# Mixing stage of an RWKV-like layer: gates made in step order inside the chunked scan, v copied through DRAM, states kept in PSUM

## The chip, the cores and the metric

One core of a Trainium2 chip runs the whole program. The metric is device time in microseconds (us) of one execution; the number for a kernel is the median of its runs. Engines: PE is TensorE (matmul), DVE is VectorE, ACT is ScalarE, POOL is GpSimd, SP is the engine that issues the transfers. SBUF is the working memory, PSUM the eight banks that matmuls write.

## The reference, cut to what matters

Inputs are 2 sequences of 1024 tokens with 128 channels, 16 heads of 8 channels. The first part ("mixing") computes, by token, projections of x mixed with the token before it, and from them gates; then a recurrence over the tokens of a sequence with one 8x8 state per head:

```
xx  = shift(x) - x ;  mix = x + xx*maa_x ;  lo = tanh(mix @ w1) @ w2 (4 parts)
xm  = x + xx*(lo + maa)                       # 4 versions: rg, wa, k, v
r, k, v, g ; w = -softplus(-(decay + w2)) - 0.5 ; a, ma, mk = sigmoid(...)
kk  = normalised(k + tanh(..)) by head ; b = -kk*a
k   = (k*ma + k*a*(1-ma)) * exp(w*mk)
step:  sa = s @ kk ;  s = s*exp(-exp(w)) + sa*b^T + v*k^T ;  y = s @ r
y   = groupnorm(y)*ln_w + ln_b + (sum r*k*faaaa)*v ;  out = (y*g) @ Wo
```

Then a layer norm, six layers of windowed attention and feed forward (the "stream"), and a last norm. Everything is float32.

## The kernel before, in words

The 2048 tokens are cut into 64 chunks (CHUNKS) of 32 steps (CHUNK). All chunks run side by side: a step of the scan works on a tile of 128 partitions (head and column) by 512 elements (8 state rows by 64 chunks). Each chunk starts from a zero state and carries two states: p=0, the state that this chunk adds, and p=1, the propagator that says what the chunk does to any start. The starts are chained afterwards. The program is a row of phases; each is a block in which every engine has its own hand-written order, with semaphores between them, and a barrier and a clearing of all the phase's semaphores (line 83) between two phases.

- **Projections** (`build_projections`). SP loads the constants; DVE, PE and ACT wait for all of them (`loaded`). Data lies by token. The matmuls follow one list `order`, in four groups of 512 tokens, over 8 PSUM banks in turn; ACT and DVE empty the banks.
- **Gates** (`build_gates`). On whole 128x2048 tiles: squares and norms of kk (line 289, 311, 331), softplus (290 to 294), a running sum of the decay by `tensor_tensor_scan` (328), decay and growth (300, 301), the gain of k (326, 341, 343, 345, 348), and the four operands of a step, `a_step`, `b_step`, `r_step`, `k_step`, rearranged from token order to step order (351 to 386). Last, 32 matmuls with `spread` (321) copy each row of v over its head's partitions, and 32 DVE products (372) make `vk`, 128 partitions by 16384 elements, the v k^T of every step.
- **Scan** (`build_scan`). 32 steps. Per step, DVE has eight instructions: `times_a` for p=0 and p=1 (line 435), `times_r` for p=1 (460), `add_vk` (441), `times_b` for both (445) and `renew` for both (454). POOL makes `times_r` for p=0 (497). PE multiplies by `headones` (`product_u`, 506) and collects y with 8 matmuls (`products_y`, 514); ACT copies y out (533). The states alternate between two SBUF tiles. A float32 matmul is two passes in the trace.
- **Mix output** (`build_mix_output`). The starts are chained, y is completed, normalised, gated and projected.
- **Stream** and **final**. Not touched by the change.

Of the kernel before, what the change touches and what calls it, by code (L numbers as in the profile page):

```python
# [21 lines left out]
F32 = mybir.dt.float32  # L22
# [68 lines left out]
def mix_inputs(sb):  # L91

    t = {}
    for name, shape in (("xT", (P, N)), ("vecs", (P, 16)), ("ident", (P, P)), ("w_lo", (P, P)), ("w_maa", (P, P)),
                        ("w_r", (P, P)), ("w_g1", (P, P)), ("w_g2", (P, P)), ("w_xwa", (P, P)), ("w_k", (P, P)),
                        ("w_xk", (P, 64)), ("w_v", (P, P)), ("w_second", (P, P)), ("w_xk2", (64, P)),
                        ("w_o", (P, P)), ("headones", (P, P)), ("spread", (P, HS * P)), ("collect", (P, HS * P)),
                        ("headmask", (P, HEADS)), ("rowmask", (P, HS))):
        t[name] = sb(name, shape)
    return t  # L100
# [3 lines left out]
V_MAAX, V_MAA, V_DECAY, V_AAAAA, V_MISCA, V_MISCK, V_FAAAA, V_LNW, V_LNB, V_ONE, V_YEPS, V_LNEPS = \  # L104
    0, 1, 5, 6, 7, 8, 9, 10, 11, 12, 13, 14

AAA_AT, MA_AT = 64, 96
MK_AT = 32


def build_projections(nc, a, t, loads, banks):

    with PhaseSignals(nc) as sems, ExitStack() as ctx:
        def sig(name, **kw):
            return Signal(sems, name, **kw)

        xx, mix, lo, gt, h1, h2 = (ctx.enter_context(nc.sbuf_tensor(n, [P, N], F32))
                                   for n in ("xx", "mix", "lo", "gt", "h1", "h2"))
        xm = [ctx.enter_context(nc.sbuf_tensor(f"xm{g}", [P, N], F32)) for g in range(4)]
        xT, vecs = t["xT"], t["vecs"]  # L120
        loaded = sig("p_loaded")
        loaded_x = sig("p_loaded_x")
        xx_made, mix_made, lo_made, gt_made = sig("xx_made"), sig("mix_made"), sig("lo_made"), sig("gt_made")
# [4 lines left out]
        a_made, ma_made, mk_made, kk_made = sig("a_made"), sig("ma_made"), sig("mk_made"), sig("kk_made")  # L128
# [18 lines left out]
        MAA, FIRST = ("maa0", "maa1", "maa2", "maa3"), ("r", "g1", "xwa", "k", "xk", "v")  # L147
        SECOND = ("g2", "z", "a", "ma", "kk", "mk")
# [12 lines left out]
        small = [n for n in loads if n != "xT"]  # L161

        @block.sync
        def _(sp):
            sp.dma_start(t["vecs"][:, :], a["vecs"]).then_inc(loaded.sem, 16)
            sp.dma_start(xT[:, :], a["xT"]).then_inc(loaded_x.sem, 16)
            for name in small:
                if name != "vecs":
                    sp.dma_start(t[name][:, :], a[name]).then_inc(loaded.sem, 16)

        @block.tensor
        def _(pe):
            pe.wait_ge(loaded.sem, 16 * len(small))
            for i, (name, j) in enumerate(order):
                w, moving, (r0, r1), ready, _ = products[name]
                pe.wait_ge(ready.sem, ready.after(j))
                if i >= 8:
                    before, at = order[i - 8]
                    freed = products[before][4]
                    pe.wait_ge(freed.sem, freed.after(at))  # L180
# [4 lines left out]
        def _(dve):  # L185
            dve.wait_ge(loaded_x.sem, 16)
            dve.wait_ge(loaded.sem, 16 * len(small))

            for s in range(B):
                lo_, hi = s * T, (s + 1) * T  # L190
                nc.vector.tensor_scalar(xx[:, lo_:lo_ + 1], xT[:, lo_:lo_ + 1], -1.0, None, ALU.mult).then_inc(xx_made.sem, 1)
                nc.vector.tensor_tensor(xx[:, lo_ + 1:hi], xT[:, lo_:hi - 1], xT[:, lo_ + 1:hi],
                                        ALU.subtract).then_inc(xx_made.sem, 1)
            dve.wait_ge(xx_made.sem, 2 * B)
            for j in range(GROUPS):
                nc.vector.scalar_tensor_tensor(out=mix[:, g_of[j]], in0=xx[:, g_of[j]], scalar=vecs[:, V_MAAX:V_MAAX + 1],
                                               in1=xT[:, g_of[j]], op0=ALU.mult, op1=ALU.add).then_inc(mix_made.sem, 1)

            def mix_in(j):

                for g in range(4):
# [4 lines left out]
                for g in (2, 3):  # L206
                    dve.wait_ge(xm_scaled[g].sem, j + 1)
                    nc.vector.tensor_tensor(xm[g][:, g_of[j]], xm[g][:, g_of[j]], xT[:, g_of[j]], ALU.add).then_inc(xm_made[g].sem, 1)
# [6 lines left out]

            for j in range(3):
                mix_in(j)
            raw_kk(0)
            mix_in(3)
            for j in range(1, GROUPS):  # L220
                raw_kk(j)

        @block.gpsimd
        def _(pool):
            for j in range(GROUPS):
# [4 lines left out]

        @block.scalar
        def _(act):
            nc.scalar.preload_act_table_set("sigmoid_and_others")
            act.wait_ge(loaded.sem, 16 * len(small))
# [8 lines left out]
                     "v": ([(t["v"], whole, ACT.Copy, None)], v_made), "g2": ([(t["g"], whole, ACT.Copy, None)], g_made),  # L243
                     "z": ([(t["z"], whole, ACT.Identity, V_DECAY), (t["w"], whole, ACT.Sigmoid, V_DECAY)], z_made),
                     "a": ([(t["a"], whole, ACT.Sigmoid, V_AAAAA)], a_made),
                     "ma": ([(t["ma"], whole, ACT.Sigmoid, V_MISCA)], ma_made),
                     "mk": ([(t["mk"], whole, ACT.Sigmoid, V_MISCK)], mk_made)}
            for name, j in order:
                if name not in reads:
                    continue  # L250
# [7 lines left out]
def build_gates(nc, t, banks, vk, last_decay):  # L258

    with PhaseSignals(nc) as sems, ExitStack() as ctx:  # L260
        def sig(name, **kw):
            return Signal(sems, name, **kw)

        vecs = t["vecs"]
        e, norm = (ctx.enter_context(nc.sbuf_tensor(n, [P, N], F32)) for n in ("gate_e", "kk_inverse"))
        gain, summed, segment, decay, growth = (vk[:, N * i:N * (i + 1)] for i in range(5))
        sq, k_step = t["xT"], t["xT"]
        squared, floored, ss_product, log_made = sig("kk_squared"), sig("floored"), sig("ss_product"), sig("log_made")
        kk_norm, kk_unit, kk_gated, soft, act_step = sig("kk_norm"), sig("kk_unit"), sig("kk_gated"), sig("soft"), sig("act_step")
        gain_made, k_scaled, key_gain, k_stepped = sig("gain_made"), sig("k_scaled"), sig("key_gain"), sig("k_stepped")  # L270
        segmented, decay_summed, decay_made, growth_made = sig("segmented"), sig("decay_summed"), sig("decay_made"), sig("growth_made")
        steps_made, v_spread, vk_made = sig("steps_made"), sig("v_spread"), sig("vk_made")
        block = ctx.enter_context(nc.Block())
        g_of = [slice(GROUP * j, GROUP * (j + 1)) for j in range(GROUPS)]
        RATE = float(np.exp(-0.5))
        PER = GROUP // CHUNKS

        def by_token(ap):

            return ap.rearrange("p (c l) -> p l c", l=CHUNK)  # L280

        def by_step(ap):

            return ap.rearrange("p (l c) -> p l c", c=CHUNKS)

        @block.scalar
        def _(act):
            nc.scalar.preload_act_table_set("natural_log_exp_and_others")
            nc.scalar.activation(sq[:, :], t["kkraw"][:, :], ACT.Square).then_inc(squared.sem, 1)
            nc.scalar.activation(e[:, :], t["z"][:, :], ACT.Abs).then_inc(act_step.sem, 1)  # L290
            act.wait_ge(act_step.sem, 1)
            nc.scalar.activation(e[:, :], e[:, :], ACT.Exp, scale=-1.0).then_inc(act_step.sem, 1)
            act.wait_ge(act_step.sem, 2)
# [1284 lines left out]
```

## Time and profile before

| | us |
|---|---|
| median of 3 runs | 2137.53 (2132.94 to 2140.84) |
| profiled execution, its own time | 2134.84 |
| span of the profiled execution | 2132.8 |
| projections, from the start to the first instruction of the gates | 69.12 |
| gates | 97.67 |
| scan | 169.66 |
| mix output | 116.64 |
| stream and final | 1679.71 |

The span is the time from the first to the last instruction; the rest of the execution's time, 2.0 us, lies around it. Phases follow each other with a barrier, so a phase that gets shorter by some time moves all that follows it by the same time.

### The profile page before, as it was taken

What the parts mean: (1) busy time and instruction counts of PE and PEld (TensorE: products, weight loads), DVE (VectorE), ACT (ScalarE), POOL (GpSimd) and SP (SyncE); (2) the same over time, 40 slices, a digit from 0 to 9 for tenths busy, and PEclk for the clock granted to TensorE, in tenths of its full rate; (3) what the DMA queues carried; (4) which work ended last, traced back from release to release, by engine and by line L of the source; (5) the groups of instructions that cost most, each with busy time, mean ns of one, the idle gap of its engine ahead of it and who ended that gap; (6) DMA issues with size and microseconds to landing.
All of it is one profiled execution on the core that took longest, in us unless ns stands there. A gap on an engine that the chain in (4) does not pass through costs nothing. (4 is left out here: it accounts for less than half of the span.)

```text
span 2132.8 us, 74062 instructions
## 1 busy us (share of the span) xinstructions
PE 1907.6 (89%) x31300; PEld 1318.9 (62%) x31300; DVE 1569.4 (74%) x2888; ACT 1221.0 (57%) x2361; POOL 1161.1 (54%) x682
## 2 busy tenths in 40 slices
PE   6576777948999999999999999999999999999984
PEld 2113556825677766667776776766777677776662
DVE  4768997347787787777877778777787777877743
ACT  4500001126677676776766767667677676776751
POOL 1401221018667666666666767666676666766630
PEclk9788998559999999999999999999999999999996
DMA  1000000033222222322223222232222322322220
GB/s 56 0 0 1 1 0 20 1 128 72 66 67 68 65 72 65 111 66 64 72 69 110 69 64 72 71 105 67 67 72 74 102 68 64 73 63 62 69 53 20
DMA packets 84859, 128.49 MB, mean 60 GB/s; under 512 B 26736, under 2 KB 32304, under 8 KB 83504
## 3 DMA queue, kind: packets, MB, share of 16 engines
q1 hardware_dynamic: 84528, 123.75, 22.8%
q8 instruction: 247, 4.05, 0.8%
q14 instruction: 84, 0.69, 0.1%
HBM read 21.94 MB, written 1.05 MB: 11 GB/s over the span
## 5 line engine op out<-in xcount | busy, mean ns | idle before, releaser
L961 POOL TENSOR_TENSOR qk<-qk,rnorm 128x1024 f32<-128x1024 f32 x192 | 361.4, 1904 | 368.9 <-ACT rnorm L1186 292.6
L955 POOL TENSOR_TENSOR qk<-qk,turnedhalf 128x1024 f32<-128x1024 f32 x192 | 454.8, 2369 | 142.8 <-DVE turnedhalf L1312 142.8
L1308 DVE TENSOR_TENSOR qk<-bank,gains 128x512 f32<-128x512 f32 x384 | 262.2, 683 | 235.1 <-ACT squares L1176 220.6
L1012 PE MATMUL bank<-wqkv,x 128*128 128x512 f32 x768 | 377.8, 595 | 22.0 <-DMA qk_gain<-in_qk_gain 20.1
L1176 ACT ACTIVATE squares<-bank 128x512 f32<-128x512 f32 x384 | 232.6, 606 | 166.0 <-PE bank L1012 163.2
L1312 DVE TENSOR_TENSOR turnedhalf<-bank,gains 128x256 f32<-128x256 f32 x768 | 285.3, 412 | 0.0
L1223 ACT ACTIVATE o_T<-bank 128x512 f32<-128x512 f32 x192 | 104.3, 599 | 229.7 <-PE bank L1076 229.6
L1318 DVE TENSOR_REDUCE rnorm<-squares 128x16 f32<-128x1024 f32 x192 | 230.6, 1201 | 2.8
L1076 PEld LDWEIGHTS bank<-p_T,v_win 64*64 64x64 f32 x12288 | 189.8, 135 | 58.0 <-issue 57.7
L1025 PEld LDWEIGHTS bank<-st_ident,qk 128*128 128x128 f32 x1536 | 179.0, 142 | 58.3 <-issue 52.2
L1017 PE MATMUL bank<-wqkv,x 128*128 128x512 f32 x384 | 202.0, 607 | 7.2 <-DVE turnedhalf L1312 6.7
L1076 PE MATMUL bank<-p_T,v_win 64*64 64x32 f32 x12288 | 201.2, 220 | 5.2 <-issue 5.1
L1025 PE MATMUL bank<-st_ident,qk 128*128 128x128 f32 x1536 | 193.6, 275 | 1.5 <-issue 1.5
L979 POOL TENSOR_TENSOR probs<-probs,total 128x1024 f32<-128x1024 f32 x96 | 183.0, 1906 | 16.2 <-DVE total L1340 16.2
L1012 PEld LDWEIGHTS bank<-wqkv,x 128*128 128x128 f32 x768 | 138.3, 191 | 84.1 <-issue 70.6
L1089 PE MATMUL bank<-o_T,wo 128*128 128x256 f32 x768 | 175.4, 382 | 2.5 <-DVE xf L1379 2.5
L1106 PE MATMUL bank<-xn_T,w 128*128 128x256 f32 (+1 forms) x576 | 163.1, 393 | 13.7 <-ACT xn_T L1242 3.3
L1089 PEld LDWEIGHTS bank<-o_T,wo 128*128 128x128 f32 x768 | 146.9, 192 | 43.1 <-issue 25.2
L1056 PE MATMUL bank<-k_T,q_T 64*32 64x64 f32 x12288 | 159.1, 225 | 15.7 <-issue 14.4
L1056 PEld LDWEIGHTS bank<-k_T,q_T 64*32 64x32 f32 x12288 | 138.9, 105 | 42.2 <-issue 39.4
L1358 DVE SCALAR_TENSOR_TENSOR ff_T<-bank,b,gate_T 128x256 f32<-128x256 f32 x144 | 64.7, 477 | 134.9 <-PE bank L1106 134.9
L1216 ACT ACTIVATE p_T<-bank 128x512 f32<-128x512 f32 x192 | 104.7, 594 | 84.8 <-PE bank L1025 84.3
(200 smaller groups left out, 3080.9 us busy)
## 6 DMA issues: line engine op xcount, KB each, us to landing
v_win<-v_tok SPq DMA_DIRECT2D x1536, 64.0 KB
wqkv<-in_wqkv SPq DMA_DIRECT2D x6, 1536.0 KB
wo<-in_wo SPq DMA_DIRECT2D x6, 512.0 KB
w<-in_w SPq DMA_DIRECT2D x6, 341.0 KB
w<-in_w SPq DMA_DIRECT2D x6, 192.0 KB
xT_sb<-in_xT SPq DMA_DIRECT2D x1, 1024.0 KB, 5.7
x_tok_sb<-in_x_tok SPq DMA_DIRECT2D x1, 1024.0 KB, 4.8
tables<-in_tables SPq DMA_DIRECT2D x2, 512.0 KB, 4.5
```

The lines of the kernel that those rows point to most:

```text
L955: nc.gpsimd.tensor_tensor(out=qk[n % 2][:, half], in0=qk[n % 2][:, half], in1=turnedhalf[:, half], op=ALU.add).then_inc(rot_added.sem, 1)
L961: nc.gpsimd.tensor_tensor(out=by_head(qk[u][:, half]), in0=by_head(qk[u][:, half]), in1=rnorm[u][:, AH * i:AH * (i + 1)].unsqueeze(2).to_b ...
L1012: nc.tensor.matmul(QK_BANKS[i][:, :], shifted_tokens(x, n, P), layer_cols(wqkv, n, 3 * INNER, 512 * i, 512), start=True, stop=True).then_i ...
L1017: nc.tensor.matmul(V_BANKS[i][:, :], shifted_tokens(x, n, P), layer_cols(wqkv, n, 3 * INNER, 2 * INNER + 512 * i, 512), start=True, stop=T ...
L1025: mm = nc.tensor.transpose(outs[i // 4][:, P * (i % 4):P * (i % 4 + 1)], source[:, P * i:P * (i + 1)], ident[:, :])
L1056: mm = nc.tensor.matmul(S_BANKS[p][at:at + WINDOW, 2 * WINDOW * a_:2 * WINDOW * (a_ + 1)], q_T[rows, a_, at:at + WINDOW], k_T[rows, a_, ke ...
L1076: mm = nc.tensor.matmul(S_BANKS[p][DH * side:DH * (side + 1), P * q + at:P * q + at + WINDOW], v_win[n % 2][rows, w, DH * a_:DH * (a_ + 1) ...
L1089: mm = nc.tensor.matmul(FF_BANK[:, 0:PT], layer_cols(wo, n, INNER, C * i, C), o_T[:, i, :], start=(i == 0), stop=(i == PAIRS - 1))
L1176: nc.scalar.activation(squares[:, 512 * i:512 * (i + 1)], QK_BANKS[i][:, :], ACT.Square).then_inc(squared.sem, 1)
L1308: nc.vector.tensor_tensor(by_head(qk[u][:, cols]), src, cos.to_broadcast([P, 8, DH]), ALU.mult).then_inc(rotated.sem, 1)
L1312: nc.vector.tensor_tensor(by_head(turnedhalf[:, cols])[:, :, to], src[:, :, frm], sin[:, :, to].to_broadcast([P, 8, half]), ALU.mult).then ...
L1318: nc.vector.reduce_sum(rnorm[n % 2][:, AH * h:AH * (h + 1)], by_head(squares[:, INNER * h:INNER * (h + 1)]), AX).then_inc(ss_made.sem, 1)
```

## The change

Everything of the mixing before the output is put in step order (chunk fastest, then step), by laying x out so on the host. Then a group of 512 columns is eight steps of all chunks (STEPS = 8), and the operands of the first eight steps can be made without the rest.

- `build_gates` goes. Its work is done by group inside `build_scan`: for group 0 ahead of the scan, and for groups 1 to 3 in between the steps of the group before (`in_step`, with a list `stages` for ACT, DVE and PE). In place of the scan over the decay (328), POOL adds the columns of one step to the next, 31 small additions of 128x64 in the projections (`sums`). The gain of k is made in the projections (`gain`), with an additional sigmoid of the negated input (`unheld`) on ACT.
- The 32 `spread` matmuls and the 32 DVE products go. v is stored to a DRAM tensor `v_dram` and read back with each row repeated over the 8 partitions of its head, 16 transfers of 128 KB per group, into `v_rep0` or `v_rep1`; POOL multiplies by k step by step (`times_k`), two steps ahead.
- In the scan the two states stay in two PSUM banks and are renewed in place. DVE loses `add_vk`; POOL adds v k to the product of b (`add_vk`), between `times_b` and `renew0`. ACT copies state 0 to SBUF for POOL's `times_r`.
- In the projections DVE, PE and ACT wait only for three loads (`FIRST_LOADS`); PE waits for the others ahead of its fifth matmul. The order of the products is changed (v first, `SECOND` = kk, a, mk, ma, z, g2). `spread`, 512 KB, is not loaded.
- In the mix output `bonus` is written by token with a stride, and two tiles take space of `v_rep0`.

```
-        small = [n for n in loads if n != "xT"]
+        rest = [n for n in loads if n not in FIRST_LOADS]
...
+            for j in range(GROUPS):
+                sp.wait_ge(v_made.sem, j + 1)
+                sp.dma_start(v_dram[:, g_of[j]], t["v"][:, g_of[j]]).then_inc(v_stored.sem, 16)
...
+                    for h in range(HEADS):
+                        rows = slice(HS * h, HS * (h + 1))
+                        sp.dma_start(v_rep[rows, :, :, :].rearrange("p i l c -> p i (l c)"),
+                                     v_dram[rows, g_of[0]].unsqueeze(0).to_broadcast([HS, HS, GROUP])).then_inc(v_copied.sem, 16)
...
+            def sums(j):
+                pool.wait_ge(z_made.sem, z_made.after(j))
+                for l in range(max(STEPS * j, 1), STEPS * (j + 1)):
+                    if l > 1:
+                        pool.wait_ge(summed.sem, l - 1)
+                    w = [t["w"][:, CHUNKS * m:CHUNKS * (m + 1)] for m in (l - 1, l)]
+                    nc.gpsimd.tensor_tensor(out=w[1], in0=w[0], in1=w[1], op=ALU.add).then_inc(summed.sem, 1)
...
 # scan, ACT
+            squares(0); absolutes(0); log_z(0); inverse_norm(0); decays(0); key_gain(0); growths(0); decays_again(0)
+            stages = ((squares, absolutes), (log_z, inverse_norm), (decays,), (), (), (key_gain,), (growths,), (decays_again,))
+            for l in range(CHUNK):
+                in_step(l, stages)
+                copy_state(l)
+                if l >= 2:
+                    read_y(l - 2)
 # scan, DVE
+            stages = ((), (), (soft_sum, unit_kk), (soft_gate, gated_kk), (soft_growth, steps_a), (steps_k,), (steps_b,), (steps_r,))
+            for l in range(CHUNK):
+                if l:
+                    times_b(0, l)
+                times_b(1, l)
+                renew1(l)
+                if l + 1 < CHUNK:
+                    times_a(1, l + 1)
+                renew0(l)
+                if l + 1 < CHUNK:
+                    times_a(0, l + 1)
+                times_r(l)
+                in_step(l, stages)
...
+            def renew0(l):
+                if l:
+                    dve.wait_ge(vk_added.sem, l + 1)
+                    dve.wait_ge(s_copied.sem, l)
+                    nc.vector.tensor_tensor(S_BANKS[0][:, :], S_BANKS[0][:, :], ubvk[:, :], ALU.add).then_inc(s_new[0].sem, 1)
 # scan, POOL
+            def add_vk(l):
+                pool.wait_ge(ub_made[0].sem, l)
+                pool.wait_ge(vk_made.sem, l + 1)
+                if l >= 2:
+                    pool.wait_ge(s_new[0].sem, l)
+                nc.gpsimd.tensor_tensor(out=rows(ubvk[:, :]), in0=rows(ub[:, 0, :]), in1=vk_of(l), op=ALU.add).then_inc(vk_added.sem, 1)
+            for l in range(CHUNK):
+                if l:
+                    add_vk(l)
+                    times_r(l - 1)
+                if l + AHEAD < CHUNK:
+                    times_k(l + AHEAD)
 # scan, PE
+            stages = ((sums_of_squares,), (), (), (), (), (), (), ())
             for l in range(CHUNK):
                 if l + 1 < CHUNK:
+                    product_u(1, l + 1)
                     product_u(0, l + 1)
                 if l:
                     products_y(l - 1)
+                in_step(l, stages)
 # mix output
-                nc.vector.tensor_tensor(bonus[:, g_of[j]], banks[4 + j % 2][:, :], t["v"][:, g_of[j]],
+                out = bonus_by_token[:, :].rearrange("p (c l) -> p l c", l=CHUNK)[:, STEPS * j:STEPS * (j + 1), :]
+                nc.vector.tensor_tensor(out, by_step(banks[4 + j % 2][:, :]), by_step(t["v"][:, g_of[j]]),
```

## Rows read from the trace of the kernel before

**Rows 1.** Busy time by phase: stretch, length, each engine's busy us (instructions), granted clock, DMA.
```profile
0.00:69.12 69.12, 44.79 (x136) 15.53 (x136) 25.83 (x36) 36.48 (x62) 10.23 (x13) 0.98 0.14 43
69.12:166.79 97.67, 60.81 (x72) 15.86 (x72) 72.82 (x49) 18.33 (x11) 24.75 (x5) 0.78 0.00 0
166.79:336.45 169.66, 125.49 (x640) 84.79 (x640) 162.38 (x260) 12.73 (x64) 41.19 (x32) 0.96 0.00 1
336.45:453.09 116.64, 89.83 (x388) 75.20 (x388) 59.81 (x169) 26.35 (x62) 11.58 (x6) 0.63 0.03 10
```

**Rows 2.** Timeline of the projections: start us, us, engine, line, what.
```profile
10.47 0.43 SPq L169 DMA_DIRECT2D rowmask_sb<-in_rowmask  x1
...
14.50 0.15 DVE L191 TENSOR_SCALAR xx<-xT_sb 128x1 f32<-128x1 f32 x1 [14.50 <-DMA rowmask_sb<-in_rowmask]
...
17.91 5.37 PE L181 MATMUL bank<-mix,w_lo_sb 128*128 128x512 f32 x8 [17.91 <-DVE mix L196]
...
64.86 0.75 ACT L255 ACTIVATE ma_sb<-bank,vecs_sb 128x512 f32<-128x512 f32 x1
65.43 0.76 ACT L255 ACTIVATE mk_sb<-bank,vecs_sb 128x512 f32<-128x512 f32 x1
69.16 2.84 DVE L326 TENSOR_SCALAR vk_sb<-a_sb 128x2048 f32<-128x2048 f32 x1 [4.34 <-PEq L83]
```

**Rows 3.** Transfers of the first 60 us: count, size, median us to landing.
```profile
xT_sb<-in_xT SPq DMA_DIRECT2D x1, 1024.0 KB, 5.7
...
w_lo_sb<-in_w_lo SPq DMA_DIRECT2D x1, 64.0 KB, 4.8
```

**Rows 4.** Groups of DVE instructions in the gates: busy us, mean ns, idle before.
```profile
L341 DVE TENSOR_TENSOR vk_sb<-vk_sb,ma_sb 128x2048 f32<-128x2048 f32 x1 | 6.7, 6652 | 0.0
...
L351 DVE TENSOR_TENSOR xT_sb<-k_sb,vk_sb 128x2048 f32<-128x2048 f32 x1 | 4.0, 4045 | 0.0
...
L336 DVE TENSOR_TENSOR gate_e<-gate_e,z_sb 128x2048 f32<-128x2048 f32 x1 | 2.3, 2293 | 0.1
```

**Rows 5.** Timeline of one steady step of the scan, DVE and POOL.
```profile
189.09 0.68 DVE L435 TENSOR_TENSOR sc_m<-sc_ahead,z_sb 128x512 f32<-128x512 f32 x1
...
191.50 1.28 DVE L445 TENSOR_TENSOR sc_ub<-bank,ma_sb 128x512 f32<-128x512 f32 x2
...
191.71 1.27 POOL L497 TENSOR_TENSOR xT_sb<-state_sb,w_sb 128x512 f32<-128x512 f32 x1 [3.69 <-DVE sc_sw L441]
192.70 0.83 DVE L454 TENSOR_TENSOR state_sb<-sc_ahead,sc_ub 128x512 f32<-128x512 f32 x1
...
194.06 0.68 DVE L435 TENSOR_TENSOR sc_m<-state_sb,z_sb 128x512 f32<-128x512 f32 x1
```

**Rows 6.** Timeline of the last step of the scan, POOL and DVE.
```profile
328.30 1.65 POOL L497 TENSOR_TENSOR xT_sb<-state_sb,w_sb 128x512 f32<-128x512 f32 x1 [1.23 <-DVE state_sb L454]
328.74 1.75 DVE L460 TENSOR_TENSOR xT_sb<-sc_ahead,w_sb 128x512 f32<-128x512 f32 x1
```

**Rows 7.** Timeline of the mix output: a matmul and its reader, two dependent DVE instructions.
```profile
354.71 3.79 PE L676 MATMUL bank<-kkraw_sb,headones_sb 128*128 128x512 f32 x8
355.77 0.69 DVE L599 TENSOR_TENSOR kkraw_sb<-bank,v_sb 128x512 f32<-128x512 f32 x1 [2.02 <-PE bank L676]
...
422.58 0.69 DVE L636 TENSOR_TENSOR z_sb<-z_sb,kkraw_sb 128x512 f32<-128x512 f32 x1
...
423.30 0.69 DVE L638 TENSOR_TENSOR z_sb<-z_sb,g_sb 128x512 f32<-128x512 f32 x1
```

**Rows 8.** Busy time at the start of the scan, columns as in the first group.
```profile
172.00:182.00 10.00, 6.90 (x8) 2.62 (x9) 7.35 (x12) 0.00 (x0) 2.48 (x2) 0.51 0.00 0
182.00:189.00 7.00, 5.83 (x37) 4.37 (x35) 6.68 (x11) 0.72 (x4) 1.33 (x2) 1.00 0.00 0
```

**Rows 9.** Groups of POOL instructions, shapes kept apart.
```profile
L379 POOL MEMSET vk_sb<- 128x64 f32 x1 | 1.2, 1170 | 0.1
L943 POOL TENSOR_TENSOR centring<-st_ident,mean_ones 128x128 f32<-128x128 f32 x1 | 0.5, 456 | 0.0
```

More of the change, by code:

```diff
@@ L199, in mix_in @@
             def mix_in(j):
-                for g in range(4):
+                for g in (3, 0, 1, 2):
                     dve.wait_ge(done[f"maa{g}"].sem, j + 1)
@@ L288, in _ @@
             nc.scalar.preload_act_table_set("natural_log_exp_and_others")
[L289 to L293, printed above, removed]
-            nc.scalar.activation(e[:, :], e[:, :], ACT.Ln, bias=vecs[:, V_ONE:V_ONE + 1]).then_inc(act_step.sem, 1)
@@ new lines, in absolutes, with log_z @@
+            def absolutes(j):
+                z = t["z"][:, g_of[j]]
+                if j:
+                    act.wait_ge(soft.sem, soft.after(j - 1, 1))
+                nc.scalar.activation(relu_z[:, :], z, ACT.Relu, scale=-1.0).then_inc(z_relu.sem, 1)
+                nc.scalar.activation(z, z, ACT.Abs).then_inc(z_abs.sem, 1)
+                act.wait_ge(z_abs.sem, j + 1)
+                nc.scalar.activation(z, z, ACT.Exp, scale=-1.0).then_inc(z_exp.sem, 1)
+            def log_z(j):
+                act.wait_ge(z_exp.sem, j + 1)
+                if j:
+                    act.wait_ge(r_made.sem, j)
+                nc.scalar.activation(Z_BANK[:, :], t["z"][:, g_of[j]], ACT.Ln, bias=vecs[:, V_ONE:V_ONE + 1]).then_inc(z_log.sem, 1)
@@ new lines, in decays, with key_gain, growths @@
+            def decays(j):
+                nc.scalar.activation(decay[:, CHUNKS + GROUP * j:CHUNKS + GROUP * (j + 1)], t["w"][:, g_of[j]], ACT.Exp,
+                                     scale=-RATE).then_inc(decay_made.sem, 1)
+            def key_gain(j):
+                act.wait_ge(soft.sem, soft.after(j))
+                nc.scalar.activation(Z_BANK[:, :], Z_BANK[:, :], ACT.Exp).then_inc(gain_made.sem, 1)
+            def growths(j):
+                act.wait_ge(k_made.sem, j + 1)
+                nc.scalar.activation(Z_BANK[:, :], t["w"][:, g_of[j]], ACT.Exp, scale=RATE).then_inc(growth_made.sem, 1)
@@ new lines, in decays_again, with copy_state @@
+            def decays_again(j):
+                act.wait_ge(b_made.sem, j + 1)
+                nc.scalar.activation(Z_BANK[:, :], t["w"][:, g_of[j]], ACT.Exp, scale=-RATE).then_inc(decay_again.sem, 1)
+            def copy_state(l):
+                if l + 1 < CHUNK:
+                    act.wait_ge(s_a[0].sem, s_a[0].after(l))
+                else:
+                    act.wait_ge(s_new[0].sem, s_new[0].after(l))
+                if l >= 2:
+                    act.wait_ge(s_r[0].sem, s_r[0].after(l - 2))
+                nc.scalar.activation(s_copy[:, l % 2, :], S_BANKS[0][:, :], ACT.Copy).then_inc(s_copied.sem, 1)
@@ new lines, in read_y @@
+            def read_y(l):
+                act.wait_ge(y_product.sem, y_product.after(l))
+                for p, y in enumerate((t["y"], t["zy"])):
+                    out = y[:, :].rearrange("p (c l) -> p l c", l=CHUNK)[:, l:l + 1, :]
+                    nc.scalar.activation(out, Y_BANKS[l % 2][:, CHUNKS * p:CHUNKS * (p + 1)].unsqueeze(1), ACT.Copy).then_inc(y_read.sem, 1)
+            squares(0)
+            absolutes(0)
+            log_z(0)
+            inverse_norm(0)
+            decays(0)
@@ L1509, in layouts @@
     out["headones"] = same.astype(f)
-    out["spread"] = np.concatenate([(same & (row == i)[:, None]).astype(f) for i in range(HS)], 1)
     out["collect"] = np.concatenate([(same & (row == i)[None, :]).astype(f) for i in range(HS)], 1)
```

535 lines of the change are left out of this document (276 added, 259 removed).

## Prediction, made before the changed kernel was run

> **What bounds the kernel now.** I read the busy time by phase first, then the timeline of each phase that the change touches. Phases are separated by barriers, so the question is what each phase costs. Gates and scan together take 267.3 of the 2132.8 us [rows 1]; 1796.4 us after them are untouched but for four instructions. No engine fills the gates: DVE is busy 72.8 of 97.7 us, PE 60.8, and they take turns. The first half is DVE beside POOL (below), the second a chain of matmul and product for vk. The reader is to see there that a DVE instruction with both inputs in SBUF, 2293 ns long by itself, took 6652 ns while POOL worked [rows 4]. In the scan, DVE is busy 162.4 of 169.7 us [rows 1]: eight instructions a step, 4.97 us from step to step [rows 5]. So DVE bounds the scan, and PE, ACT and POOL have room. The projections start late: DVE's first instruction at 14.50 us was released by the last of all loads [rows 2], and ACT is the last engine to end, at 66.19, 2.9 us before the gates.
>
> **Projections.** Three loads are needed instead of all. xT lands 5.7 us and w_lo 4.8 us after its issue [rows 3]; issued first and third (about 0.74 and 1.7), both are there by about 6.9. From DVE's start to PE's first matmul were 3.4 us [rows 2]; with xx made by group these are an edge, 448 columns (0.6) and one mix (0.75), about 2.1. PE starts at 9.0 instead of 17.91: -8.9. The other loads had landed by 14.5 [rows 2] and the first four matmuls take 5.4 us, so PE's new wait ahead of its fifth costs nothing. ACT has one sigmoid more per group; two starts are 0.57 apart [rows 2], and only in the last two groups does ACT run without a gap: +1.0, less 0.4 since v no longer waits in the line. POOL's sums are new: 128x128 took 456 ns [rows 9] and 128x512 1.27 us [rows 5], so 0.0021 us an element and about 0.32 for 64, with the handoff to itself 0.4. The first three groups lie beside other work; the last eight, 3.2 us, start after w's last sigmoid, 0.6 before ACT ends: +2.6. Bounds: 0.3 each gives +1.8; the one POOL instruction on 64 columns took 1170 ns [rows 9], beside a DVE instruction, and at that price groups 2 and 3 both run late, +13. I take 0.4, since nearer shapes say so. Six more semaphores to clear: gaps of 1.3 us after the scan (14 semaphores) and 2.9 after the projections (42, [rows 2]) say 0.06 each, +0.4. Together -5.3; the scan's phase begins at 63.8 instead of the gates' at 69.12.
>
> The stores and copies of v are out of the way, I think. SP has nothing else to issue in either phase; a load of 1 MB landed in 5.7 us [rows 3]. Group 0's 2 MB have over 40 us, group 1's are needed six steps into the scan (some 43 us), those of groups 2 and 3 are released when the steps that read the buffer are done and have seven steps (36 us) each. If the 16 transfers of a group came one after another at 5.7 us each, they would need 91 us: rival 4.
>
> **Gates in front of the scan.** Only 512 columns are made ahead: ACT table load 1.3; square, Relu, Abs, Exp, Ln at 0.57 to 0.6 (3.1); the floor, Ln and Exp of the norm (1.9, dependent) and the decay (0.6); then DVE's steps_a, times_a, gated_kk, steps_k (2.6), growth on ACT and steps_b (1.3), decay again and steps_r (1.4), with 1.5 us of handoffs between them and for the cold square-sum matmul: 12.7 us to the first `times_b`. The price of the small DVE instructions is that of 128x512 with a PSUM input, 0.69 [rows 7]. This replaces 97.67 us and some 3 us of setting up the scan.
>
> **The steady step.** Let T be the end of `times_b` for p=0. On DVE independent instructions start 0.60 apart, dependent ones 0.72 [rows 5, 7]. `times_b` p=1 starts at T-0.09, renew1 at T+0.64, `times_a` p=1 at 1.37 to 2.06, renew0 at 1.97 to 2.66, `times_a` p=0 at 2.70 to 3.39. PE takes it 0.06 later, and its reader starts 1.06 after the matmul [rows 7]: the next `times_b` starts at 4.51 and ends at 5.20. `times_r` fits before it (3.30 to 3.99). So the period is 5.20, set by the loop through PE, and DVE idles 0.5 us, against 4.97 before. The wait that the change adds, renew0 on POOL's `add_vk`: POOL starts 0.13 after its input and takes 1.27 [rows 5], done at T+1.40, while renew0 can't start before 1.97 in DVE's order: nothing, by 0.57 us. Behind renew0 are queued `times_a` p=0 and with it everything; each us beyond that cover costs a us per step. POOL's three instructions take 4.0 of 5.2 us. PE's y matmuls (2 us) wait for POOL's `times_r`, end at T+6.3 and are not needed by the `product_u` of the next step before T+7.3. ACT's copy of the state has 3 us of slack.
>
> The gates of the next group are nine DVE instructions: none in two steps of eight, one in three (0.60, it fills the idle 0.5), two in three (+0.6 each). Three groups: 9 x 0.6 = +5.4. At the start PE's granted clock is 0.5: before, it was so for some 15 us of thinly used PE, and 1.00 from 182 on [rows 8]; the first three steps cost 5.5, 6.6 and 7.1 instead of 5.2, +3.6. So 31 x 5.20 + 5.4 + 3.6 = 170.2 us from the first step to the last, 7.4 to the last read of y, and 2.8 for the barrier (39 semaphores). The phase takes 12.7 + 170.2 + 7.4 + 2.8 = 193.1 instead of 267.3: -74.2. Bounds of the period: 4.8 if the loop through PE is 0.4 shorter (the second pass overlaps more), -12; the upper is the writing of PSUM by DVE, which no row shows. Reading PSUM costs nothing that the rows show (`times_b` from a bank starts its twin 0.60 later, like the others). The nearest row of a slowed instruction is a renewal of 0.83 against 0.68 [rows 5]; 0.15 on the six instructions of the loop is 0.9 a step, +28. I take no surcharge, since `times_b` is nearest.
>
> The page "VectorE: DVE Perf Modes" of the Trainium skill (section "The TRN2 errata — SBUF-src ops pay a fixed extra latency per instruction") speaks against states in PSUM: it gives a DVE instruction that reads PSUM 120 cycles of fixed cost against 58 from SBUF. At its 0.96 GHz that is 0.065 us, on six instructions 0.39 a step, an estimate of +12 for the scan. The trace doesn't agree: two `times_b`, which read a bank, take 1.28 together [rows 5].
>
> **Mix output.** The four bonus products are written with a stride. A fully strided instruction took 4045 against 2293 ns [rows 4], so 0.3 more per 512 columns: +1.2.
>
> **Sum.** -5.3 - 74.2 + 1.2 = -78.3, from the profiled execution's own 2134.84: 2056.5. The median of the runs is 2.7 above that execution; I put half of it on top: **2058**.
>
> **The rivals.**
> 1. Forecast, 2058, own range 2045 to 2072. Chance 0.68.
> 2. DVE pays for PSUM operands, or the loop is longer by as much: from 2058 + 12 (0.4 a step) to 2058 + 28. For it: nobody wrote PSUM from DVE in this scan; against: `times_b`. 2070 to 2086, chance 0.14.
> 3. POOL's sums cost 1.2 us each, +10: 2068. For: the 1170 ns row; against: DVE held POOL there. Or the v copies are some us late in each group. Chance 0.10.
> 4. The other side: POOL and DVE exclude each other. POOL now works 4 of 5.2 us in the scan, and in the last step before, both slowed each other, 1.65 against 1.27 and 1.75 against 0.68 [rows 6]. If they took strict turns, a step would be 4.6 us of DVE plus 3.8 of POOL, 8.4: +99 on 31 steps, 2157. It decides from 7.7 us a step (78.3/31 more than 5.2). Against it: two `times_b`, one input in a bank, ran under POOL's 1.27 without getting longer [rows 5], and now each DVE instruction of a step has an input in a bank. The same sign comes from v copied one transfer at a time, 91 us a group against some 40, three times 50. Together 0.05.
> 5. Faster than my range: the period is 4.6 (DVE's own sum) and the projections save more, 2036. Chance 0.03.
>
> Beyond the ends of the range lies about 0.1 on each side: 2044 to 2086. What a measurement here can tell from no change is 0.5%, 11 us: faster 0.93, within it 0.02, slower 0.05.
>
> **What would show it.** First PE matmul at 9 us; the scan's phase from 64 to 257; first `times_b` 13 us into it; 5.2 us steady steps in the last eight, with DVE waiting for PE ahead of `times_b` p=0 and not for POOL ahead of renew0; renew0 and renew1 at 0.69; POOL at 1.27; the stream as long as before. A wait for POOL at renew0, renewals over 0.75, or a DMA releasing `times_k` would make it wrong.

## The result, and the profile after

| | before | after |
|---|---|---|
| median of the runs, us | 2135.24 (2125.82 to 2140.84, 4 runs) | 2053.78 (2050.26 to 2054.72, 4 runs) |
| profiled execution, its own time | 2134.84 | 2050.26 |
| projections | 69.12 | 66.86 |
| gates and scan | 267.33 | 193.95 |
| mix output | 116.64 | 118.43 |
| stream and final | 1679.71 | 1669.26 |

The ratio is 0.962, 95% interval 0.9582 to 0.9658: faster, and 2053.78 lies 4.2 below the forecast of 2058. The busy time by phase of the kernel after answers to [rows 1]; the four rows are projections, scan with its gates, mix output, and stream with final.

```profile
0.00:66.86 66.86, 45.11 (x136) 15.38 (x136) 37.46 (x53) 39.66 (x65) 23.30 (x43) 0.95 0.42 84
66.86:260.81 193.95, 141.41 (x646) 86.90 (x646) 168.62 (x262) 57.31 (x145) 118.06 (x95) 0.92 0.25 33
260.81:379.24 118.43, 90.20 (x388) 75.41 (x388) 60.78 (x169) 26.32 (x62) 11.57 (x6) 0.62 0.03 10
379.24:2048.50 1669.26, 1582.03 (x30064) 1122.41 (x30064) 1248.83 (x2374) 1126.06 (x2163) 1073.01 (x627) 0.98 0.29 74
```

DVE's 168.6 busy us of 193.95 say that it is nearly full and yet not the only bound. The mixing ends at 379.24 instead of 453.09, which is -73.85 where the forecast's sum had -78.3. The other -10.4 of this pair of profiles lie in the stream, whose code is the same; what they are, the first experiment tells.

The timeline of the projections of the kernel after, the same places as [rows 2]:

```profile
6.07 0.15 DVE L202 TENSOR_SCALAR vecs_sb<-vecs_sb 128x1 f32<-128x1 f32 x1 [6.07 <-DMA w_lo_sb<-in_w_lo]
...
8.01 2.90 PE L196 MATMUL bank<-x,w_lo_sb 128*128 128x512 f32 x3 [8.01 <-DVE x L213]
...
58.73 1.15 ACT L306 ACTIVATE g_sb<-bank 128x512 f32<-128x512 f32 x1
59.02 3.97 POOL L271 TENSOR_TENSOR w_sb<-w_sb 128x64 f32<-128x64 f32 x8 [0.72 <-ACT w_sb L313]
66.94 0.11 DVE L468 MEMSET decay<- 128x64 f32 x1 [6.50 <-PEq L83]
```

DVE starts when w_lo is there, and PE 9.9 us earlier than before. But ACT ends at 59.88, only 6.3 earlier: it needs 49.7 us from its first `lo` (10.16) to its end, against 46.1 before. POOL's last sums end later still, at 62.99, and the barrier takes the rest. Two groups of ACT instructions say why ACT needs longer, the copy of g that is now written with a stride and the additional sigmoid (`unheld`, which lies in the tile `x`); the third line is the copy of g in the kernel before:

```profile
L306 ACT ACTIVATE g_sb<-bank 128x512 f32<-128x512 f32 x4 | 4.5, 1118 | 0.0
L302 ACT ACTIVATE x<-bank,vecs_sb 128x512 f32<-128x512 f32 x4 | 2.8, 696 | 0.0
```

```profile
L255 ACT ACTIVATE g_sb<-bank 128x512 f32<-128x512 f32 x4 | 2.4, 603 | 0.3
```

One steady step of the scan, timeline of the kernel after (it answers to [rows 5]). L531 is `times_b`, L526 `times_a`, L537 `renew0`, L544 `renew1`, L551 `times_r`; L597 is POOL's `add_vk`, L633 PE's `product_u`:

```profile
218.68 1.29 DVE L531 TENSOR_TENSOR sc_ub<-bank,mk_sb 128x512 f32<-128x512 f32 x2 [0.62 <-PE bank L633]
219.45 1.27 POOL L597 TENSOR_TENSOR sc_ubvk<-sc_ub,v_rep 128x512 f32<-128x512 f32 x1 [1.57 <-DVE sc_ub L531]
220.01 0.70 DVE L544 TENSOR_TENSOR bank<-bank,sc_ub 128x512 f32<-128x512 f32 x1
220.68 1.27 POOL L604 TENSOR_TENSOR sc_m<-sc_copy,r_sb 128x512 f32<-128x512 f32 x1
220.74 0.69 DVE L526 TENSOR_TENSOR sc_m<-bank,z_sb 128x512 f32<-128x512 f32 x1
221.35 0.69 DVE L537 TENSOR_TENSOR bank<-bank,sc_ubvk 128x512 f32<-128x512 f32 x1
...
222.07 0.69 DVE L526 TENSOR_TENSOR sc_m<-bank,z_sb 128x512 f32<-128x512 f32 x1
222.68 0.68 DVE L551 TENSOR_TENSOR sc_m<-bank,r_sb 128x512 f32<-128x512 f32 x1
...
222.82 1.12 PE L633 MATMUL bank<-sc_m,headones_sb 128*128 128x512 f32 x2 [0.21 <-DVE sc_m L526]
...
223.98 0.69 DVE L531 TENSOR_TENSOR sc_ub<-bank,mk_sb 128x512 f32<-128x512 f32 x1 [0.62 <-PE bank L633]
```

Read it as a loop: `times_b` p=0 (218.68), its `renew0` (221.35), `times_a` p=0 (222.07), the matmul (222.82), the next `times_b` (223.98). The period is 5.30. The only wait of DVE is for PE, 0.62. POOL's sum `add_vk` is ready at 220.72, 0.63 before `renew0` starts. Groups of DVE instructions in the scan's phase, mean ns of one:

```profile
L531 DVE TENSOR_TENSOR sc_ub<-bank,mk_sb 128x512 f32<-128x512 f32 x63 | 40.6, 684 | 11.2 <-PE bank L633 10.9
L544 DVE TENSOR_TENSOR bank<-bank,sc_ub 128x512 f32<-128x512 f32 x32 | 22.4, 700 | 1.1
...
L537 DVE TENSOR_TENSOR bank<-bank,sc_ubvk 128x512 f32<-128x512 f32 x31 | 21.4, 690 | 0.1
```

A renewal, which reads a bank and writes one, takes 690 to 700 ns; `times_b`, which only reads one, takes 684.

A step did not get shorter: 5.30 us against 4.97 in the kernel before. The phase without its front takes 181.5 us, the scan before took 169.66. So all of the 73.4 us that gates and scan became shorter come from the gates, 97.67 us before and now 12.5 in front of the first `times_b` and some 5 inside the steps (gates_ahead below). No run gave DVE its `add_vk` back or kept the `spread` matmuls and their products; how the gain divides among these edits is not shown.

### The profile page after: what moved, and what is told of

Its sections match the earlier page's. It is cut to its first block and busy times, and to the rows that moved or that the text cites. A ratio compares the mean times of both kernels' runs of the same rounds, so it can differ in the third digit from the quotient of the medians.

```text
span 2048.5 us, 74276 instructions
## 1 busy us (share of the span) xinstructions
PE 1858.8 (91%) x31234; PEld 1300.1 (63%) x31234; DVE 1515.7 (74%) x2858; ACT 1249.4 (61%) x2435; POOL 1225.9 (60%) x771
```

## The experiments

Each is the kernel after with one edit, but for the first (none) and for v_16_twice, best and best2 (several). The scan's phase is from its first instruction to the first of the mix output.

**before_again and after_again: both kernels once more, in rounds.** No edit.

> The kernel before once more. The stretch from the start of the stream to the end was 1679.7 us in the first trace of before and 1669.3 in that of after, with the same instructions. If this is a spread between executions, this trace shows another length of that stretch, somewhere from 1665 to 1690, with the mixing as before (453.1 to 1 us). If instead the change made the stream shorter, this trace shows 1679.7 within 2 us again.

> The changed kernel once more. The mixing ends again at 379.2 within 1 us. Spread theory: the stretch after it differs from 1669.3 by some us either way. Rival (the change shortens the stream): 1669.3 within 2 us.

Measured: the kernel before 2137.61 us (ratio to itself 0.9994, 0.9974 to 1.0014), the kernel after 2060.31 us, ratio 0.9623 (0.9578 to 0.9667). In the profiled executions the stream took 1678.3 and 1679.0 us; the scan's phase of the kernel after took 192.72, from 66.47 on. Windows of the second profile of the kernel after:

```profile
66.47:259.19 192.72, 141.12 (x646) 86.64 (x646) 168.47 (x262) 57.31 (x145) 118.01 (x95) 0.92 0.26 33
377.49:2056.50 1679.01, 1588.84 (x30064) 1127.53 (x30064) 1248.38 (x2374) 1125.97 (x2163) 1072.79 (x627) 0.98 0.29 74
```

What follows: before_again alone came out as its rival had it (1678.3 is within 2 us of 1679.7); after_again decides, since the same kernel's stream now took 9.8 us more than in its first profile. The mixing repeats within 1.8 us, not within the 1 us expected. The stream's 1669.26 was the shortest of fourteen profiles (the thirteen others: 1672.8 to 1682.6), and in the second pair the stream was no shorter with the change. So the 10.4 us are spread between executions; that a part of a few us is not, these profiles can't exclude. In the second pair the mixing is 76.0 us shorter (it ends at 453.5 and 377.5).

**all_loads: DVE waits for every load again.**

```
             dve.wait_ge(loaded_first.sem, 16 * len(FIRST_LOADS))
+            dve.wait_ge(loaded.sem, 16 * len(rest))
```

> Undoes the early start alone: DVE's first instruction waits for all loads again. My theory: the last load lands at about 12.9 us (issue at 9.6, 2.8 to landing), DVE starts there and not at 6.1, and all of the 6.8 us reach the start of the scan's phase, 73.7 instead of 66.9. Rival (PE or ACT bound the projections, the early start is absorbed): 67 to 70.

Measured: 2062.73 us, ratio 0.9651 (0.962 to 0.9683). DVE's first instruction, timeline:

```profile
13.03 0.15 DVE L203 TENSOR_SCALAR vecs_sb<-vecs_sb 128x1 f32<-128x1 f32 x1 [13.03 <-DMA rowmask_sb<-in_rowmask]
```

PE starts at 14.97 instead of 8.01, and the scan's phase begins at 72.65 instead of 66.86: of 7.0 us at the start 5.8 reach the end of the projections, nearer to the theory's 73.7 than to the rival's 67 to 70. So in the traces the short list of loads is worth some 6 us, more than all that the projections won (2.26). The totals can't tell it (2060.31 for the kernel after in the same round, and the intervals overlap).

**pool_twice: POOL makes v k plus the product twice.**

```
+                nc.gpsimd.tensor_tensor(out=rows(ubvk[:, :]), in0=rows(ub[:, 0, :]), in1=vk_of(l), op=ALU.add).then_inc(once.sem, 1)
+                pool.wait_ge(once.sem, l)
                 nc.gpsimd.tensor_tensor(out=rows(ubvk[:, :]), in0=rows(ub[:, 0, :]), in1=vk_of(l), op=ALU.add).then_inc(vk_added.sem, 1)
```

> POOL makes the sum of v k and the product of b twice in each of 31 steps, one after the other, so vk_added comes 1.26 us later. My theory, the addition is hidden behind DVE's order with 0.6 us to spare: the period goes from 5.30 to 5.96, the scan's phase gets 20 us longer (31 x 0.66). Rival (the addition is already what renew0 waits for): +1.26 a step, +39. Rival (the loop is not through POOL at all): below +3.

Measured: 2089.15 us, ratio 0.9768 (0.9729 to 0.9806), 28.8 more than the kernel after in the same round; scan's phase 221.2, +27.2. The timelines of DVE and of POOL in one step:

```profile
214.72 1.27 POOL L598 TENSOR_TENSOR sc_ubvk<-sc_ub,v_rep_sb 128x512 f32<-128x512 f32 x1 [1.47 <-DVE sc_ub L532]
216.06 1.26 POOL L600 TENSOR_TENSOR sc_ubvk<-sc_ub,v_rep_sb 128x512 f32<-128x512 f32 x1
...
217.36 0.70 DVE L538 TENSOR_TENSOR bank<-bank,sc_ubvk 128x512 f32<-128x512 f32 x1 [0.67 <-POOL sc_ubvk L600]
...
227.01 1.29 DVE L532 TENSOR_TENSOR sc_ub<-bank,mk_sb 128x512 f32<-128x512 f32 x2 [0.97 <-PE bank L636]
```

POOL's second sum adds 1.34, of which the cover of 0.63 hides a part and `renew0` waits 0.67. The undisturbed step is 6.06, +0.76, where the theory had +0.66; 31 steps make 23.6, where it had 20. So the theory is nearer than its rivals, +39 and below +3. Of the other 3.6 us, 1.4 lie in the last step, where DVE has no `times_a` ahead of `renew0`, which waits 1.39 for POOL. The other 2.2 lie in the steps, and go with PE's granted clock: it was 0.89 from 216 to 232 and 0.91 from 232 to 250, where the kernel after had 1.00, and the step that ends at 227.01, with 0.97 of waiting for PE, took 7.01. That the clock made these steps long is read from the trace, no run held it. POOL's own instructions stay at 1.27 with DVE at work all along, so the two don't take turns (the prediction's fourth rival).

**gates_ahead: all four groups of gates before the first step,** on ACT, DVE and PE (the same for DVE's and PE's lists):

```
-            squares(0)
...
-            decays_again(0)
-            stages = ((squares, absolutes), (log_z, inverse_norm), (decays,), (), (), (key_gain,), (growths,), (decays_again,))
+            for j in range(GROUPS):
+                for stage in (squares, absolutes, log_z, inverse_norm, decays, key_gain, growths, decays_again):
+                    stage(j)
+            stages = ((),) * STEPS
```

> The gates of all four groups are made ahead of the first step, with the same instructions, none in the scan. My theory, each group is a chain of 9.0 us between ACT and DVE (from its Ln to steps_r, as group 0 shows), and in the scan it costs only 3 x 3 x 0.6 us of DVE: +27 ahead, -5.4 in the steps, the scan's phase +22. Rival (the gates in the steps cost DVE their full 27 x 0.6 = 16 us, or delay the loop): +27 - 16 = +11 or less.

Measured: 2080.07 us, ratio 0.9739 (0.9721 to 0.9756); scan's phase 218.18, +24.2. The first `times_b` comes 41.6 us into the phase instead of 12.5; the rest takes 176.6 instead of 181.5. Hence three groups of gates cost 29 us in front of the scan (theory 27) and 5 inside it. They fit there because DVE has 0.62 idle in a step: a step with one of their DVE instructions still takes 5.30, one with two takes 5.78 at full clock. A third of the gain on gates and scan (24.2 of 73.4) would be lost without this overlap.

**v_twice: every copy of v a second time, into a tile that nobody reads.**

```
...
+                    sp.dma_start(dump[part, :, :, :].rearrange("p i l c -> p i (l c)"),
+                                 v_dram[part, g_of[j]].unsqueeze(0).to_broadcast([HS, HS, GROUP])).then_inc(v_again.sem, 16)
```

> Each copy of v for groups 1 to 3 is made twice, the second time into a tile that nobody reads, so the transfers' traffic in the scan doubles. My theory, the copies have over 10 us of slack in every group: the same steps, scan's phase within 1 us. Rival (the copies are just in time, or slow other things down in SBUF): times_k waits for a DMA at steps 6, 14 or 22, over 3 us each.

Measured: 2130.01 us in one execution, some 75 more; scan's phase 270.6, +76.6. The theory (within 1 us) failed, and its rival came true: three waits of over 20 us each. What POOL waited for, in total, times, longest:

```profile
POOL v_rep L596 <- DMA v_rep<-v_by_step: 49.3, 2, 28.2
POOL v_rep_sb L596 <- DMA v_rep_sb<-v_by_step: 30.6, 1, 30.6
```

Windows of the kernel after, while the copies of group 1 run and behind them (the last two columns are DMA share and GB/s):

```profile
66.86:99.90 33.04, 17.88 (x50) 8.31 (x50) 24.05 (x38) 15.62 (x27) 13.07 (x11) 0.68 0.51 64
99.90:121.94 22.04, 17.81 (x80) 11.26 (x80) 21.23 (x35) 5.33 (x15) 14.32 (x13) 0.92 0.00 1
```

A group's 2 MB take 31 to 33 us, at 64 GB/s and with half of the DMA engines' time. Group 3 was issued at 166.13, had landed at 197.1 and was first read at 206.01: 9 us of slack. Group 2 had less: the last of its bytes moved at 155.2 and it was first read at 161.98, some 6 us. Group 1 had 18 (99.9 and 117.79). Doubling the copies uses all of it up. The prediction had put this cost among the hidden ones by the rate of another transfer; it was hidden, but just.

**v_16 and v_16_twice: 8 copies of 256 KB over all partitions in place of 16 over 8,** and the same doubled as above (into the unread tile).

```
-                for h in range(HEADS):
-                    part = slice(HS * h, HS * (h + 1))
-                    sp.dma_start(vk[j % 2][part, :, :, :].rearrange("p i l c -> p i (l c)"),
-                                 v_dram[part, g_of[j]].unsqueeze(0).to_broadcast([HS, HS, GROUP])).then_inc(v_copied.sem, 16)
+                for i in range(HS):
+                    sp.dma_start(vk[j % 2][:, i, :, :].rearrange("p l c -> p (l c)"), spread_row(v_dram, i, j)).then_inc(v_copied.sem, 16)
```

where `spread_row` takes row i of each of the 16 heads and repeats it over the head's 8 partitions; the copies of group 0 in the projections likewise.

> The kernel after, with each group's 2 MB of v copied by 8 transfers of 256 KB, each over all 128 partitions (outermost dimension 16 heads), instead of 16 transfers of 128 KB, each over 8 partitions. Theory (the copies after run on half of the DMA engines, share 0.53, 31 us a group, because the outermost dimension is 8): the share while they run is near 1.0 and a group lands 15 to 18 us after its first issue; SP's wait for group 3 falls from 23 us to 8 to 10. The step doesn't depend on it: the scan's phase stays at 193 to 195 us and the whole within 0.5% of after. Rival (the DRAM side or the small rows set the rate): 28 to 33 us a group and a share that rises without the rate rising.

> The same as v_16, and every copy of groups 1 to 3 issued a second time into a tile that nobody reads. The doubled copies at half the engines cost +75 us in the scan's phase, by POOL's wait at times_k. Theory (the missing engines were the reason, and there is now twice the slack): a doubled group lands in 30 to 36 us, as a single one did after, and the scan's phase stays within 3 us of 194. Rival (the rate is set by something else than the number of engines): again +50 to +75 us, POOL's times_k released by DMA.

Measured: 2062.29 and 2055.73 us, one execution each; scan's phase 193.10 and 193.59. Windows of v_16 during the copies of group 3, and one of v_16_twice at the same place:

```profile
168.00:172.00 4.00, 2.79 (x17) 1.77 (x16) 3.90 (x7) 1.75 (x4) 3.31 (x3) 1.00 0.91 191
172.00:176.00 4.00, 3.77 (x20) 2.46 (x20) 3.31 (x7) 1.54 (x5) 2.43 (x3) 1.00 0.85 165
```

```profile
178.00:182.00 4.00, 3.46 (x20) 2.24 (x18) 3.30 (x6) 2.46 (x6) 2.43 (x3) 1.00 0.86 193
```

The rate goes from 64 GB/s to between 165 and 193 and the share from 0.53 to some 0.9; group 3 lands 14.3 us after its issue instead of 31. Doubled copies now cost nothing (76.6 us of the scan's phase before): POOL waits for no DMA, and a doubled group 3 lands 24.1 us after its issue, where 30 to 36 were expected. The time doesn't fall by it, since the copies were hidden; the slack grows. That the old copies left half of the DMA engines idle agrees with a rule of the Trainium skill ("DMA: Bandwidth & Descriptors", section "Rules for kernel authors"): an outermost dimension of c below 16, a broadcast of c copies for instance, confines a transfer to at most c engines. Here c was 8. The rate rose by almost three and not by two, which the rule doesn't explain; the transfers were also half as many and twice as long, and no run parts the two.

**p0_first: p=0 is served first,** since the loop goes through it (PE's two `product_u` likewise).

```
                 renew1(l)
-                if l + 1 < CHUNK:
-                    times_a(1, l + 1)
                 renew0(l)
                 if l + 1 < CHUNK:
                     times_a(0, l + 1)
+                    times_a(1, l + 1)
```

> DVE renews state 0 and multiplies it by a before it does so for state 1, and PE takes the product of p=0 first; no instruction more or less. My theory, the period of 5.30 is the loop b, renew1, a1, renew0, a0, PE: with a1 out of the loop it ends 0.5 earlier, 4.8 in steps without gates, 5.25 and 5.85 in those with one or two of their instructions: the scan's phase -7.6 us. Now renew0 starts when POOL's sum arrives, with no cover left. Rival (POOL's sum, or PE's second product, is then as late as what it replaces): -1 to +3.

Measured: 2051.62 us, ratio 0.9609 (0.9586 to 0.9631); scan's phase 185.77, -8.2. Timeline of one step of DVE and POOL:

```profile
213.39 0.69 DVE L531 TENSOR_TENSOR sc_ub<-bank,mk_sb 128x512 f32<-128x512 f32 x1
...
214.16 1.27 POOL L596 TENSOR_TENSOR sc_ubvk<-sc_ub,v_rep 128x512 f32<-128x512 f32 x1 [0.99 <-DVE sc_ub L531]
214.25 0.69 DVE L531 TENSOR_TENSOR sc_ub<-bank,mk_sb 128x512 f32<-128x512 f32 x1 [0.17 <-PE bank L632]
...
215.58 0.69 DVE L537 TENSOR_TENSOR bank<-bank,sc_ubvk 128x512 f32<-128x512 f32 x1
...
218.21 0.69 DVE L531 TENSOR_TENSOR sc_ub<-bank,mk_sb 128x512 f32<-128x512 f32 x1
```

A steady step takes 4.82; DVE idles 0.17 and POOL's sum is ready 0.15 before `renew0`. The order of two independent instructions was worth 0.48 a step. Over 31 steps that would be 14.9 us; only 8.2 came, because DVE has no idle time left for the gates: with one of their instructions a step now takes 4.98 to 5.20, with two 5.64 to 5.80 instead of 5.78. The theory's -7.6 had counted this. Now DVE, POOL's sum and the loop lie within 0.2 us of each other.

**best, best2 and z_early: p0_first with more, and one part alone.** best adds a reordered list of products and moves the load of ACT's table from the start of the scan to the end of the projections. best2 moves the table load too, keeps the old list and adds the copies of v_16. z_early is the kernel after with the new list alone.

```
-        SECOND = ("kk", "a", "mk", "ma", "z", "g2")
+        SECOND = ("kk", "z", "a", "ma", "mk", "g2")
...
+            nc.scalar.preload_act_table_set("natural_log_exp_and_others")
```

> p0_first, with the product z second in the line of the second products (so w's last sigmoid, on which POOL's last eight sums wait, comes four ACT instructions earlier, 2.3 us) and the scan's table load at the end of ACT's work in the projections. My theory: -7.6 in the scan as p0_first, -1.3 for the table load, and -1.4 in the projections, where DVE's last gain then ends last: -10 in all against the changed kernel, about 2043 to 2050. Rival (barriers wait for something else than POOL): -8.

> The kernel after with p=0 served first (renew0 and times_a p=0 before times_a p=1), the copies on 16 engines and ACT's table loaded at the end of the projections, the second list of products in the order of after. Theory: the scan's phase is 8.2 us shorter by the order of the step and up to 1.3 by the table, and begins as after, at 66.9 or 1.3 later by the table in ACT's line; with both, -8 to -9.5 us to the end of the scan and a ratio of 0.959 to 0.960 to before. Rival (the table load only moves, ACT being last to end in the projections): as p0_first alone, -8.2.

> The kernel after with only the second list of products reordered: kk, z, a, ma, mk, g2 (z second instead of fifth). Meant to let POOL's last eight sums start earlier: if that was right and the table load was what lengthened the projections of the combined kernel, the scan's phase begins at 65.5. Rival, now the likelier: the order itself costs PE and ACT about 3 us (z's reader is slow and holds up the banks behind it), so ACT ends at 62 to 63 and the phase begins at 66.8 to 68.5 with nothing gained.

Measured: best 2050.56 us, ratio 0.9603 (0.9586 to 0.9621); best2 2052.67 us, ratio 0.963 (0.96 to 0.9661); z_early 2057.86 us in one execution. The scan's phase begins at 68.05 in best and 67.68 in z_early (after: 66.86), but at 65.77 in best2. What ACT waits for between 20 and 66 us in z_early:

```profile
ACT z_sb L313 <- PE bank L196: 2.7, 3, 0.9
```

In the kernel after, ACT doesn't wait for z's bank at all, and its last gap, 0.26, ends at 39.28. With z second, ACT waits 0.9 in each of three groups for z's product and ends at 62.68 instead of 59.88. The same list in best does the same (ACT's last copy ends at 62.94), so the idea of an earlier w failed by the list and not by the table load: the phase did not begin at 65.5, and z_early came out as its rival had it. How much the list costs is less sure, as the kernels with the old list began the phase between 65.77 and 67.68. In best2 the first `times_b` comes 11.2 us into its phase, 1.3 less than after: the table is off the path. The scan nevertheless ends at 252.40, where p0_first ended at 252.65, and not 2.4 us earlier. Windows of two steps at the same place in best2 and in p0_first:

```profile
191.51:203.22 11.71, 8.64 (x38) 5.40 (x37) 10.25 (x18) 2.48 (x8) 7.45 (x6) 0.85 0.01 1
```

```profile
193.07:203.47 10.40, 6.93 (x38) 4.80 (x37) 10.15 (x17) 2.48 (x8) 7.46 (x6) 1.00 0.01 2
```

The same number of PE instructions took 8.64 us busy at a granted clock of 0.85, and 6.93 at 1.00, and the two steps were 1.3 us longer. So the start that was won at the front was given back in places like this one. PE's timelines there, best2 and then p0_first:

```profile
195.06 3.66 PE L632 MATMUL bank<-sc_m,headones_sb 128*128 128x512 f32 x4 [2.03 <-DVE sc_m L526]
```

```profile
196.62 1.98 PE L632 MATMUL bank<-sc_m,headones_sb 128*128 128x512 f32 x4 [2.03 <-DVE sc_m L526]
```

In both PE had been idle for 2.03 us. In best2 the granted clock then stood at 0.50, which is 1.2 GHz, the lower of its two levels, until 198.6; in p0_first it stayed at 1.00, and the same four matmuls took 1.98 us instead of 3.66. best has three long steps at the same places of the scan as best2 (6.55, 6.46 and 6.60 us where p0_first has 5.80, 5.80 and 5.21; best2 6.56, 6.50 and 6.66), and p0_first has one of 6.24 elsewhere. Why the clock fell after one such idle stretch and not after another stays open. In the totals none of these versions can be told from the kernel after (intervals from 0.9586 to 0.9661, those of the kernel after 0.9578 to 0.9667), and both expectations of the total were just missed: 2043 to 2050 for best, 0.959 to 0.960 for best2. In the traces they can: the scan's phase took 185.8 to 186.6 us in the three kernels with p=0 first, and 192.7 to 194.5 in six profiles with the old order, nothing added to the step and no wait for copies.

## Why the prediction was right, step by step

- **The whole.** 2058 was forecast, 2053.78 measured, 2060.31 on another occasion. Forecast for the mixing -78.3, measured -73.85 (-76.0 in the second pair). The stream's spread more than made up for the difference in the first profile, which is luck; the forecast's mechanism stands, and its sum was 4.4 us too good: 3.0 in the projections, 0.85 in the scan's phase, 0.6 in the mix output.
- **Projections, -5.3 forecast, -2.26 measured.** This is the term that was off by most. PE started at 8.01 (forecast 9.0), since the loads were there at 6.07 and not 6.9: 1.0 better. That "only in the last two groups does ACT run without a gap: +1.0, less 0.4" failed: ACT's part is 3.6 us longer, 3.0 worse. Its busy time rose by 3.2 [rows 1]. Four added sigmoids start 0.57 apart, 2.3 us. `g_sb` is written by token with a stride, 1118 ns in place of 603 in the trace before. From its start to the next are 0.84 to 0.86; before, 0.48 in the one group where ACT did not wait for PE behind it (62.67 to 63.15), so some 1.4 more in four groups. Both together are 3.7. ACT's idle time in this stretch hardly changed, so nearly all of it counts. The stride of `g_sb` was not in the sum at all, though that of `bonus` was. The attribution is read from the trace; no run took the stride away.
- **POOL's sums, +2.6 forecast for the last eight, +3.1 measured:** 0.50 each, against 0.4. The 1170 ns row [rows 9] was no price of this instruction. The barrier took 3.87 instead of 2.93, 0.9 more where +0.4 had been forecast.
- **Gates in front, 12.7 forecast, 12.5 measured.** This is luck in part: the terms that the prediction lists (1.3, 3.1, 1.9, 0.6, 2.6, 1.3, 1.4, 1.5) add up to 13.7.
- **The steady step, 5.20 forecast, 5.30 measured.** The order of events was as forecast (`renew0` 1.98 after T, `times_a` p=0 at 2.70, PE at 3.45), and DVE waits for PE and not for POOL. The 0.10 is the matmul and its reader: 1.16 apart (222.82, 223.98), not the 1.06 of [rows 7].
- **Later gates and start, +5.4 and +3.6 forecast.** From the first to the last step it took 171.7 us, forecast at 170.2. The 0.10 a step would give 3.1 more, so these two terms were 1.6 too high together. At full clock the nine steps with two gate instructions take 0.48 more than 5.30 each, 4.3 where 5.4 was forecast. The remaining 3.1, by the starts of `renew1`, lie in steps with a mean granted clock of 0.65 to 0.76: 2.1 in the first two (6.22 and 6.52), and 1.0 in three later ones (6.23, 6.14, 5.96), which the forecast did not have; it had put its 3.6 into the first three steps.
- **States in PSUM cost nothing: right.** 690 to 700 ns a renewal, against 683 ns for an instruction of the stream with a bank as input and SBUF as output, and independent ones start 0.60 apart as before. The estimate of +12 from the Trainium skill ("VectorE: DVE Perf Modes", section "The TRN2 errata — SBUF-src ops pay a fixed extra latency per instruction") was not borne out by this trace.
- **POOL beside DVE: right.** POOL 1.27, DVE 0.69 while overlapping, pool_twice too. The Trainium skill ("SBUF — State Buffer", section "Who interferes with whom") has it that a DVE instruction with at most one SBUF input doesn't contend with GpSimd, outside the perf modes that use two ports; every DVE instruction of the step has one input in a bank, so the trace agrees.
- **Copies of v "out of the way": right in effect, without the measure.** The load of 1 MB in 5.7 us [rows 3] was no price for them: 2 MB took 31 to 33 us. A margin of some 6 us in group 2 and 9 in group 3 held.
- **Mix output, +1.2 forecast, +1.8 measured:** a strided product of `bonus` took 1036 ns in the mean of four instead of 691 in the trace before, 1.4 for the four. The prediction's own rows (4045 against 2293 ns for 2048 columns) give 0.44 for 512 and not the 0.3 that it used; measured were 0.35. Groups of DVE instructions of the mix output, after and before:

```profile
L725 DVE TENSOR_TENSOR a_sb<-bank,v_sb 128x512 f32<-128x512 f32 x4 | 3.8, 1036 | 2.3 <-PE bank L802 2.3
```

```profile
L599 DVE TENSOR_TENSOR kkraw_sb<-bank,v_sb 128x512 f32<-128x512 f32 x4 | 2.8, 691 | 2.7 <-PE bank L676 2.7
```

## What to carry to other kernels

When work is moved off one engine, follow the loop through the others with starts, not durations, and find the slack behind each new wait; here POOL's sum was ready 0.63 us early, DVE had 0.62 idle in a step for the gates, and the tightest copy had some 6 us. Put the instruction on the loop first: in the traces an order was worth 8 us of the scan at no cost. Ask of every transfer that should be hidden how many DMA engines it uses, and price strided writes on each engine that got one.

## What the runs showed of the hardware

- Copies with an outermost dimension of 8 ran at 64 GB/s and a DMA share of 0.53 (after); with one of 16, and half as many transfers, at 165 to 193 GB/s and some 0.9 (v_16, v_16_twice).
- ACT writing 128x512 with a stride: 1118 ns, without one 603. DVE with a bank read and a strided write: 1036 against 691 ns.
- PE's granted clock dips in the scan, in places that differ between kernels and were the same in best and best2 (0.89 from 216 to 232 in pool_twice, 0.85 from 191.5 to 203.2 in best2), with longer steps, up to 7.01 instead of 6.06 us. After the same 2.03 us of idle PE it stood at 0.50 in best2 and at 1.00 in p0_first.
- The stream, the same code in all fourteen profiles, took between 1669.3 and 1682.6 us.
